# A mixture-of-experts layer: pairs of experts ordered so that neighbours share one, rows packed without gaps, and each tile's sum kept in SBUF

## What is computed

```python
x = L0_attn_x
xn = _layernorm(x, axis=-1)
x = x + _L0_attn_ref(xn, ...) + _L0_ffn_ref(xn, ...)
# _L0_ffn_ref, with 2 shared experts, 8 routed experts, hidden width 256:
_ffn = lambda x, w1, w2, w3: jax.nn.silu(x @ w1.T) * (x @ w3.T) @ w2.T
shared = _ffn(xf, sw1[0], sw2[0], sw3[0]) + _ffn(xf, sw1[1], sw2[1], sw3[1])
logits = xf @ router_w.T + expert_bias
rw, sel = jax.lax.top_k(logits, 2)          # each token's two experts
rw = jax.nn.softmax(rw)
out = shared + sum over the token's two experts of rw * _ffn(xf, expert)
```

## Time and profile before

| | |
|---|---|
| median of 3 runs | 502.98 us (502.68 to 503.12) |
| the profiled execution, its own time | 503.18 us |
| its span, first to last instruction | 501.4 us |
| PE busy | 432.6 us (86%) |
| DVE busy | 331.3 us (66%) |
| ACT, POOL busy | 229.1 us, 231.1 us |
| routed stage | from 262.43 us on |

### The profile page before, as it was taken

The page is one execution under the profiler, slowest core; times in us unless marked ns, Lnnn a source line. Parts: engine busy times, 40 slices in busy tenths (PEclk is TensorE's granted clock), DMA queues, the critical chain, the costliest instruction groups (busy, mean ns, idle before and its releaser), DMA issues.

```text
span 501.4 us, 14718 instructions
## 1 busy us (share of the span) xinstructions
PE 432.6 (86%) x5200; PEld 376.1 (75%) x5200; DVE 331.3 (66%) x956; ACT 229.1 (46%) x432; POOL 231.1 (46%) x179
## 2 busy tenths in 40 slices
PE   0167676677899999999999999999999999999990
PEld 0156534354577777777788999999999999999990
DVE  3799799989768799999966776344434444344440
ACT  0588841163224544444443454444444444444440
POOL 0234400146754433333000000688888888887663
PEclk9999998999999999999998999999999999999995
DMA  8999400000331111111302432354444444432000
GB/s 238 284 171 174 74 1 1 5 32 18 99 112 34 54 44 55 48 43 48 96 2 96 140 110 95 75 59 64 63 55 66 55 60 60 60 37 23 4 2 1
DMA packets 50683, 34.58 MB, mean 69 GB/s; under 512 B 9408, under 2 KB 44224, under 8 KB 50624
## 3 DMA queue, kind: packets, MB, share of 16 engines
q1 hardware_dynamic: 32048, 23.88, 20.4%
q0 software_dynamic: 15296, 8.53, 12.4%
q10 hardware_dynamic: 3280, 1.36, 1.1%
HBM read 14.87 MB, written 20.69 MB: 71 GB/s over the span
## 4 chain that ended last, share of the span: by engine, by line
PE 72%; DVE 19%; issue 2%; ACT 2%; ACTq 2%; DMA 1%; POOL 1%; DVEq 0%; POOLq 0%
PE pY L616 17%; PE pY L466 9%; PE pAB L596 9%; PE pAB L598 8%; PE pAB L597 8%; PE pAB L451 4%; PE pAB L453 4%; PE pAB L452 4%; PE pV L491 3%; PE pV L478 3%; DVE units L894 3%; PE pV L579 2%; DVE hbuf L923 2%; DVE hot L834 2%; ACTq L630 2%
## 5 line engine op out<-in xcount | busy, mean ns | idle before, releaser
L798 POOL DMA_INDIRECT out_dram<-hot,rows x92 | 142.5, 1549 | 110.9 <-DVE hot L1173 86.0
L1167 DVE SCALAR_TENSOR_TENSOR hbuf<-pAB,units 128x512 f32<-128x512 f32 x92 | 63.6, 691 | 103.9 <-PE pAB L598 103.9
L596 PE MATMUL pAB<-xT,wsp 128*128 128x128 f16 x736 | 129.6, 220 | 1.1 <-ACT xT L737 0.6
L597 PE MATMUL pAB<-xT,wsp 128*128 128x128 f16 x736 | 129.7, 220 | 0.0
L598 PE MATMUL pAB<-xT,wsp 128*128 128x128 f16 x736 | 129.6, 220 | 0.0
L788 POOL DMA_INDIRECT sorted_rows<-rows,slot x64 | 69.4, 1084 | 112.2 <-DVE hbuf L923 64.4
L616 PE MATMUL pY<-wsp,hbuf 128*128 x736 | 103.0, 282 | 1.0 <-issue 0.7
L747 ACT ACTIVATE units<-pAB 128x512 f32<-128x512 f32 x92 | 55.0, 598 | 105.5 <-PE pAB L598 105.5
L616 PEld LDWEIGHTS pY<-wsp,hbuf 128*128 128x128 f32 x736 | 89.7, 192 | 1.7 <-issue 1.3
L701 ACT ACTIVATE units<-pAB 128x512 f32<-128x512 f32 x64 | 38.1, 597 | 113.8 <-PE pAB L453 113.8
L596 PEld LDWEIGHTS pAB<-xT,wsp 128*128 x736 | 72.5, 98 | 2.6 <-issue 2.1
(11 more groups left out here) (137 smaller groups left out, 558.0 us busy)
## 6 DMA issues: line engine op xcount, KB each, us to landing
sorted_rows<-c_pad_row SPq DMA_DIRECT2D x1, 6026.0 KB, 43.7
rows<-sorted_rows SPq DMA_DIRECT2D x46, 131.0 KB, 2.2
base<-in_x SPq DMA_DIRECT2D x4, 1024.0 KB, 8.2
out_dram<-base SPq DMA_DIRECT2D x16, 256.0 KB, 2.5
wraw<-in_wall SPq DMA_DIRECT2D x8, 256.0 KB
out_dram<-hot,rows POOLq DMA_INDIRECT x92, 3.3
sorted_rows<-rows,slot POOLq DMA_INDIRECT x64
wsp<-in_wall SPq DMA_DIRECT2D x8, 128.0 KB, 2.8
```

The costliest lines, as they stand in the source:

```text
L596: pe.matmul(o, hi, x(0), start=True, stop=False)
L597: pe.matmul(o, hi, x(1), start=False, stop=False)
L798: pool.indirect_dma_start(out_rows, bass.IndirectOffsetOnAxis(ap=xr[:, t // 2 % X_RING, t % 2, DEST:DEST + 1].bitcast(U32), axis=0), yt[:, ...
L1167: v.scalar_tensor_tensor(hbuf[:, r % 4, :], pAB[:, 2 * (r % 2) + 1, :], 1 / (XS * WS), silu[:, r % 2, :], ALU.mult, ALU.mult).then_inc(d_h ...
```

## The change

Pairs are put in an order (`RUNS`) in which each differs from the one before it by one expert. Rows are packed without gaps: 64 full tiles. A tile's two experts are those of the pair of its first row, so a tile in which a new pair begins also needs the expert that comes in (`COMER`): 27 extra single-expert products, one at each border, run two to a job in 14 extra jobs (the last one has one expert). So there are 78 jobs, with the extras after the first 8 tiles. A row now carries its 8 combine weights (137 words, 131 before); for each tile DVE works out which weights its two experts get (`side_products`, `side_sums`), and an extra is multiplied by 0 where its border does not exist. The sums of all 64 tiles stay in SBUF (`yt` in the space of `xT`, cleared by 16 memsets on POOL), and DVE adds both halves of each job. POOL makes 64 sends in place of 92, none before the last extra is added. The write of empty rows goes.

```diff
-PAIRS = [(u, v) for u in range(E) for v in range(u + 1, E)]
+RUNS = [(0, 1, 8), (1, 7, 8), (1, 2, 7), (2, 6, 8), (2, 3, 6), (3, 5, 8), (3, 4, 5), (4, 5, 8), (5, 7, 8), (5, 6, 7), (6, 7, 8)]
+PAIRS = [(u, v) for u, lo, hi in RUNS for v in range(lo, hi)]
-TILES = -(-((TOK + NPAIR * (P - 1)) // P) // 2) * 2
+EXTRAS = NPAIR - 1
+TILES = NT
+XTILES = (EXTRAS + 1) // 2
-ADDS = 3
+ADDS = 2
+EXTRA_FROM = 8
+JOBS = ([Job(t=t) for t in range(EXTRA_FROM)] + [Job(i=i) for i in range(XTILES)]
+        + [Job(t=t) for t in range(EXTRA_FROM, TILES)])
...
-            sp.dma_start(sorted_rows.rearrange("(t p) w -> p t w", p=P),
-                         c["pad_row"][:].unsqueeze(1).broadcast_to([P, TILES, ROWW])).then_inc(pad_out, 16)
...
+            def spread_sides():
+                pe.wait_ge(spread_ready, 1)
+                pe.wait_ge(y_read, NB)
+                for b in range(2):
+                    mm = pe.matmul(pY[:, b, :], c["ones"][:], spread.rearrange("p t m -> p (t m)")[:, b * BLK:(b + 1) * BLK],
+                                   start=True, stop=True)
+                mm.then_inc(sides_done, 1)
...
             def r_second(g, r):
-                t = UNROLL * g + r
-                pe.wait_ge(d_hf, t + 1)
+                q = UNROLL * g + r
+                job = JOBS[q]
+                pe.wait_ge(d_hf, q + 1)
-                if t >= 2:
-                    pe.wait_ge(d_y, t - 1)
+                if q >= 2:
+                    pe.wait_ge(d_y, q - 1)
...
-            pipeline(act, TILES, UNROLL, TILES // UNROLL, [(0, r_xt), (5, r_y_first), (2, r_silu)])
+            pipeline(act, NJOB, UNROLL, NJOB // UNROLL, [(0, r_xt), (2, r_silu)])
...
+            pool.wait_ge(cw_pair, 1)
+            for m, (choice, k) in enumerate(((5, 8), (4, 9))):
+                nc.gpsimd.tensor_tensor(r8[:, choice], r8[:, choice], rt[:, k, :].unsqueeze(2).broadcast_to([P, NT, E]),
+                                        ALU.mult).then_inc(cw_part, 1)
+            pool.wait_ge(cw_part, 2)
+            nc.gpsimd.tensor_tensor(rows32[:, :, CW:CW + E], r8[:, 5], r8[:, 4], ALU.add).then_inc(cw_ready, 1)
...
+            for i in range(NB):
+                pool.wait_ge(l1, 4 * i + 4)
+                nc.gpsimd.memset(yt[:, TPB * i:TPB * (i + 1)], 0.0).then_inc(y_cleared, 1)
...
+                pool.wait_ge(d_y, max(job.place, LAST_EXTRA) + 1)
...
+            def y_first(g, r):
+                job = JOBS[UNROLL * g + r]
+                q = job.place
+                dve.wait_ge(d_l2, q + 1)
+                if job.main:
+                    dve.wait_ge(share_ready, job.step + 1)
+                    v.scalar_tensor_tensor(yt[:, job.t], pY[:, q % 2, 0:P], share_w[:, job.t, 0:1], yt[:, job.t],
+                                           ALU.mult, ALU.add).then_inc(y_half, 1)
...
+            def y_second(g, r):
+                dve.wait_ge(y_half, q + 1 if q <= LAST_EXTRA else q)
+                if job.main:
+                    v.scalar_tensor_tensor(yt[:, job.t], pY[:, q % 2, P:2 * P], share_w[:, job.t, 1:2], yt[:, job.t],
+                                           ALU.mult, ALU.add).then_inc(d_y, 1)
...
-            pipeline(dve, TILES, UNROLL, TILES // UNROLL, [(0, r_attention), (5, r_y), (2, r_hf)])
+            extra_tile = load_tiles(1, 15) | load_tiles(15, NPAIR)
+            pipeline(dve, NJOB, UNROLL, NJOB // UNROLL, [(0, r_attention), (5, y_first), (2, r_hf), (5, y_second), (2, side_products),
+                                                         (3, side_sums), (2, extra_shares)])
```

More of the change, by code:

```diff
@@ L269, in layer_kernel @@
         const_in = sem("const_in")
-        pad_out = sem("pad_out")
         w_split_hi = sem("w_split_hi")
@@ L341, in layer_kernel, with rows_landed, rows16_of @@
         sorted_steps = sorted_rows.rearrange("(s k p) w -> s p k w", k=2, p=P)
+        sorted_tiles = sorted_rows.rearrange("(t p) w -> t p w", p=P)
         out_rows = out.rearrange("b s c -> (b s) c")
+        def rows_landed(eng, step):
+            n = TURN_ORDER.index(step)
+            before = sum(1 if s < MAIN_STEPS else min(2, EXTRAS - 2 * (s - MAIN_STEPS)) for s in TURN_ORDER[n % AHEAD:n + 1:AHEAD])
+            eng.wait_ge(d_in[n % AHEAD], 16 * before)
+        def rows16_of(job, k):
+            return xr16[:, job.step, k] if job.main else xe16[:, 2 * job.i + k]
         block = ctx.enter_context(nc.Block())
@@ L570, in r_turn @@
                     return
-                j = UNROLL // 2 * g + r // 2
-                pe.wait_ge(d_in[j % AHEAD], 16 * (j // AHEAD + 1))
-                if j == 0:
+                rows_landed(pe, job.step)
+                if job.turn == 0:
                     pe.wait_ge(w_split, NE)
-                if past(j, 2):
-                    pe.wait_ge(d_xt, j - 1)
-                for k in range(2):
+                if job.turn >= 2:
+                    pe.wait_ge(d_xt, job.turn - 1)
+                for k in range(2 if job.main else job.experts):
@@ L586, in r_first @@
-                if t >= 2:
-                    pe.wait_ge(d_hf, t - 1)
+                q = UNROLL * g + r
+                job = JOBS[q]
+                pe.wait_ge(d_xt, job.turn + 1)
+                if q >= 2:
+                    pe.wait_ge(d_hf, q - 1)
                 else:
                     pe.wait_ge(hf_done, UNITS)
-                x = lambda s: xrT[:, r // 2, r % 2, s, :]
-                for bank, col, done in ((2 * (r % 2), W1, d_a), (2 * (r % 2) + 1, W3, d_l1)):
-                    for k in range(2):
+                for bank, col, done in ((2 * (q % 2), W1, d_a), (2 * (q % 2) + 1, W3, d_l1)):
+                    for k in range(job.experts):
+                        x = lambda s: xrT[:, job.turn % RING, job.t % 2 if job.main else k, s, :]
@@ L1170, in r_y, with load_tiles @@
-            def r_y(g, r):
-                t = UNROLL * g + r
-                dve.wait_ge(d_first, t + 1)
-                v.scalar_tensor_tensor(yt[:, t % Y_RING], pY[:, r % 2, P:2 * P], xr32[:, t // 2 % X_RING, t % 2, CW + 1:CW + 2], yt[:, t % Y_RING],
-                                       ALU.mult, ALU.add).then_inc(d_y, 1)
+            straight(UNITS - ROUND, UNITS + 4, both + [(0, spread_out, UNITS - ROUND, UNITS)])
+            def load_tiles(first, last):
+                _, tiles = nc.values_load_multi_w_load_instructions(
+                    segi[0:1, 1, first:last], engines=(mybir.EngineType.DVE,), min_val=0, max_val=TILES - 1,
+                    skip_runtime_bounds_check_because="clamped")
+                return dict(zip(range(first, last), tiles))
@@ new lines, in side_sums, with extra_shares @@
+            def side_sums(g, r):
+                job = JOBS[UNROLL * g + r]
+                if job.main and job.turns:
+                    dve.wait_ge(side_parts, job.step + 1)
+                    v.tensor_reduce(share_w[:, 2 * job.step:2 * job.step + 2], side_scr[:, job.step % 2], AX.X, ALU.add).then_inc(share_ready, 1)
+            def extra_shares(g, r):
+                job = JOBS[UNROLL * g + r]
+                if job.main:
+                    return
+                rows_landed(dve, job.step)
+                for k in range(job.experts):
+                    a = 2 * job.i + k + 1
+                    v.tensor_tensor(extra_w[:, a:a + 1], xe32[:, a - 1, CW + COMER[a]:CW + COMER[a] + 1], active[:, a:a + 1],
+                                    ALU.mult).then_inc(extra_parts, 1)
```

361 lines of the change are left out of this document (239 added, 122 removed).

## The result

The changed kernel takes **572.66 us** (median of 4 runs, 571.98 to 573.5), the kernel before 503.05 us on the same chip: ratio 1.1385, 95% interval 1.1365 to 1.1405, so 14% slower. The profiled execution took 573.17 us, its span 571.3. The prediction was 555 us, from 545 to 575.

The account below looks back on a forecast made before the run. TensorE and VectorE waiting for each other were to set the routed stage's pace: r_hf of job 3 at 275.6, 74 jobs x 3.61 = 267.1, half job -2.5, then the tail, 8.65 and 1.8, giving 554.8 us; range 545 to 575.

Parts of the forecast that it names:

- closed round: Routed stage: TensorE cannot go on until VectorE has done r_hf and y_second; 3.61 us a job, 1.19 more than 2.42.
- still about 1 us a job: Sign in the profile after: VectorE's wait for first products in the routed stage stays about 1 us a job.
- The order does not hold TensorE: Rival, routed stage: y_second is over before TensorE comes, pace stays 2.42 us, GpSimd's sends end it at 470 us; chance 0.07.
- TensorE's own issue: Rival, routed stage: address instructions show after each wait, at most 0.3 us a main tile, 19 us in all, 574 us; chance 0.13.
- Slower by the clock: Rival, routed stage: idle TensorE drops to clock 0.50, round 5.8 us for a third of the jobs, some 610 us; chance 0.04.
- GpSimd's memsets run then too, behind the last scatter: Near unit 61, ahead of the routed stage: the memsets' end is needed only some 10 us into the stage.
- VectorE's 27 register loads: Start of the routed stage: up to 2.7 us, ending before r_hf of job 0; taken as 0, bound 2.
- Routing: Ahead of the routed stage: VectorE drops weight operations and small ones, gains a larger table and pair products; net -1.0 us.
- contention: Routing: GpSimd's three weight products beside VectorE slow its operations; 0.5 us taken, bounds 0 and 3.4.
- Unit 61's extra work: Near unit 61: VectorE gets a 1024-element product and eight small operations, 2.8 us partly idle; 1.0 taken, bounds 0 and 2.8.
- `spread_sides`: Start of the routed stage: TensorE's two wide products for the side weights wait for the last shared sum; +0.5 us.
- The tail: End of the kernel: GpSimd has caught up and sends at 544.4, after the last sum at 544.2; + 8.65 gives 553.0.

Follow-up runs that it names:

- more work in the round: Changed kernel with VectorE's y_first moved behind r_hf as well, ahead of y_second: 602.76 us, ratio 1.1979.
- the run with the loads taken apart: Changed kernel with VectorE's 27 register loads moved from the start of the routed stage into the extra jobs that need them: 565.61 us, ratio 1.1242.
- the kernel before with the moved entry: Kernel before the change with only r_y moved behind r_hf in VectorE's list: 617.01 us, ratio 1.226.
- the last experiment: Changed kernel, y_second before r_hf, memsets spread, register loads in jobs, three attention blocks a job; then GpSimd's routing-weight products wait until slots are ready: 470.49 us.
- the run with the order alone: Changed kernel with one entry of VectorE's list moved, y_second ahead of r_hf instead of behind it: 485.53 us, ratio 0.9652.

## Why the prediction was right, and where it was 18 us short

**The mechanism and its size were right.** The prediction's closed round, 3.61 us a job with legs of 0.95, 1.28, 0.28, 0.61, 0.34 and 0.15, measured 3.62 with nearly the same legs. One of its signs was wrong: VectorE's wait for first products is not "still about 1 us a job" but 2.1, nearer to the 2.5 that its own working had. Moving the one entry takes the hold away (572.66 to 485.53), moving it in the kernel before brings it there (503 to 617), and more work in the round lengthens it by just that work. That is shown, not argued.

**The rivals.** "The order does not hold TensorE" is out for the kernel as it was changed; with the order mended the time went below its 501 us, to 485.53 (it had put 470 there, with sends from about 350 us; they started at 359). "TensorE's own issue", 574 us, came close in time for other reasons. Its 0.3 us a main tile isn't there: the pace is 3.62 for main and extra jobs alike, though only main jobs have address instructions. Only the register loads show: with an empty queue one opened a gap of 6.28 and one of 4.51 us between two `r_hf`, 3.5 us above two rounds, and 1.3 of that is the low clock behind the first. In the order that keeps TensorE fed the same two gaps are 3.17 and 2.53, where 2.29 or 2.51 is normal. "Slower by the clock" did not happen as the rival had it: 1.00 from 350 to 400 us with TensorE busy 73% of the time, with a pause of about 1 us in each job. It fell for a few us behind one of TensorE's register loads (idle 1.11 us more) and behind the late start of the stage (idle 2.8 us). The first row is the gap of 6.28 us, the second the start, the third the first row's gap in the run with the loads taken apart:

```profile
407.61:413.89 6.28, 4.20 (x35) 3.59 (x32) 1.30 (x5) 1.18 (x2) 5.37 (x4) 0.77 0.57 66
280.00:284.00 4.00, 3.74 (x32) 3.66 (x33) 1.94 (x8) 0.60 (x1) 0.00 (x0) 0.66 0.23 79
401.72:406.68 4.96, 2.94 (x35) 2.40 (x32) 1.30 (x5) 1.18 (x2) 4.04 (x4) 1.00 0.45 60
```

The pauses of the first and the third are nearly the same, so what decides is not shown. The prediction's argument against this rival was thinner than it looked: the stretch from 12.5 to 50 us, "19.92 of 37.5 us busy and yet granted 1.00", was granted 0.82 in the changed kernel (busy 18.06), and also in the kernel before with the moved entry (busy 18.79), whose code up to there is that of the kernel before.

**What the sum missed**, in the profiled execution (span 571.3 against 553.0):

| term of the sum | predicted | measured | difference |
|---|---|---|---|
| `r_hf` of job 3 | 275.6 | 286.9 | +11.3 |
| job 3 to job 77 | 264.6 | 269.4 | +4.8 |
| job 77 to the last send | 4.2 | 8.1 | +3.9 |
| last send to the end | 8.65 | 6.9 | -1.7 |

- *Ahead of the stage.* The prediction had +1.0 us for everything; it became +12.3 (274.62 to 286.89). Of this 0.6 is there at the first shared unit, 1.3 come with the routing work by unit 12, 6.1 with the memsets by the last unit, and 4.3 between the last unit and job 3. The step that failed outright is "GpSimd's memsets run then too, behind the last scatter; their end is needed only some 10 us into the stage". It asked when their result is needed, and not what they do to VectorE while they run, although the row on such a neighbour stood beside the contention term.
- *VectorE's 27 register loads*, "0, bound 2". The price per register was taken from waits of TensorE, at most 0.5 us for 5. But such a wait shows what was left of a load after queued products had covered it. A load in the open costs 0.24 us a register, 6.51 in all. The prediction had no row of its own for it.
- *Routing*, -1.0, with *contention* of 0.5 within 0 to 3.4: from the first shared unit to unit 12 it became +1.3 together. The contention is 0.96 on one operation, within its bounds, and moving the products away gained nothing, as the last experiment shows. Of the gain of 1.0 little shows: in the run with the order alone, where VectorE paid 0.5 for the contention, these units still took 0.1 more than before, which leaves about 0.4. The row that the prediction read for its rule on two inputs is an operation with one tensor and two scalars; the 128x1792 sum, with two tensors, is what bears it out. *Unit 61's extra work*, 1.0: the last unit is late by 8.0 us and unit 60 was by 7.9, so 0.1. *`spread_sides`*, 0.5: nothing can be seen in the 16.9 us of the run without the loads.
- *In the stage* 74 rounds were 0.015 us longer each (1.1 us) and the register loads of TensorE added 3.5, the low clock behind one of them included; the half job saved 2.6 where 2.5 was put.
- *The tail* took GpSimd to be free at the last sum. It was one send behind each of the last sums, which come 0.7 to 1.3 us apart.

The range held because the issue rival had stretched it to 575 us; the likeliest case's own upper end, 565, did not hold.

## What to carry to other kernels

Where an engine's list has an instruction that signals standing behind one that waits, follow both engines' lists once around: if the two ends wait for each other, the pace is the sum of the legs, whatever share of time each engine is idle, and an entry moved by one place can be worth more than all the work that a change saves. Price a background operation by what it does to its neighbour while it runs, not only by when its result is needed. Price an instruction that blocks a sequencer from a place where nothing covers it.

## What the runs showed of the hardware that was not expected

- GpSimd's memsets, which read nothing, kept VectorE's 16-bit `TENSOR_SCALAR` operations out for a whole row of them: 6.16 us beside fifteen of 0.54, 7.97 beside sixty of at most 0.23, and 0.70 beside a single one, where 0.62 is normal. The Trainium skill (SBUF — State Buffer, Who interferes with whom) says that VectorE in a two-port mode and GpSimd exclude each other for a whole instruction. The trace agrees that one blocks the other fully; but the hold lasts here for the whole row of instructions, not for one. As each memset is recorded to begin before the one ahead has ended, the runs don't tell whether VectorE is passed over or nothing is ever given free. Its 32-bit `hf_unit` with a source in PSUM was not held beside the same memsets (0.69 us).
- Which engine starts first decides who pays most. In one execution of the changed code GpSimd's product was first and VectorE's operation took 2.98 us; in the run with the order alone VectorE was first (2.15 us), and the product took 2.93 instead of 1.27. VectorE's next operation of this size then took 2.37 where 2.02 is normal, so it paid 0.5 us in place of 0.96. Unit 6 came 1.3 us sooner, counted from the first unit; 0.5 of that is a shorter wait for TensorE ahead of the sum (1.08 us against 1.61), which is also what let VectorE be first.
- A register load from SBUF costs 0.24 us a register on VectorE. The Trainium skill (Runtime: NRT & Kernel Launch, Instruction fetch mechanics) gives about 0.2 us per register for loads from HBM at launch; no trace here has one of those, and the price from SBUF is near it.
